# Ranks from one sum of one-hots, places by ScalarE's adding passes, in a graph layer's sorting kernel

## The reference

```python
h    = relu(layernorm(x)) @ W_in2f.T
W    = (smu(edge_attr @ W_f1.T + b_f1) @ W_f2.T + b_f2) * edge_weight[:, None]
agg  = segment_sum(h[dst] * W, src, 12500)
out  = x + smu(agg @ W_o1.T + b_o1) @ W_o2.T + b_o2
```

## Time and profile before

| | |
|---|---|
| median of 3 timed runs | 4130.89 us (4128.15 to 4133.09) |
| the profiled execution's own time | 5828.1 us, which is its span; no time around it is given |
| TensorE products busy in the span | 4390.8 us (75%), 32406 products |
| VectorE busy | 3425.3 us (59%) |
| ScalarE busy | 2120.4 us (36%) |
| GpSimd busy | 3041.4 us (52%) |
| mean granted TensorE clock | 0.825 of full |

### The profile page before, as it was taken

How to read it: one execution, slowest core, us unless ns; L and a number is a source line. 1 busy time by engine, 2 the same in 40 slices (tenths; PEclk the granted TensorE clock), 3 DMA queues, 4 the chain that set the end, 5 groups by cost and what they waited for, 6 DMA issues and landing times.

```text
span 5828.1 us, 115538 instructions
## 1 busy us (share of the span) xinstructions
PE 4390.8 (75%) x32406; PEld 3600.8 (62%) x32406; DVE 3425.3 (59%) x11901; ACT 2120.4 (36%) x7301; POOL 3041.4 (52%) x3173
## 2 busy tenths in 40 slices
PE   5566557777777777777777777777778788778888
PEld 4455446666666666666666666666666666666667
DVE  6555455555565555555555555555656666566667
ACT  3455333333333333333333333333333333333332
POOL 4555555555555555555555555555555555555552
PEclk8777778787888888888788888888888888888899
DMA  5354334444443433433333333333444444445547
GB/s 163 105 134 136 111 109 130 132 130 130 131 122 108 116 112 112 115 115 112 110 113 112 117 112 112 112 111 115 129 132 133 136 141 138 136 135 146 153 143 198
DMA packets 460270, 736.98 MB, mean 126 GB/s; under 512 B 87920, under 2 KB 256218, under 8 KB 459856
## 3 DMA queue, kind: packets, MB, share of 16 engines
q1 hardware_dynamic: 292358, 461.45, 29.9%
q0 software_dynamic: 100000, 206.60, 10.6%
q10 hardware_dynamic: 67626, 65.48, 3.4%
HBM read 465.36 MB, written 267.82 MB: 126 GB/s over the span
## 4 chain that ended last, share of the span: by engine, by line
another core or an unknown queue 34%; PE 32%; issue 14%; DVE 9%; ACT 8%; ACTq 2%; DMA 1%; DVEq 1%; SPq 0%; POOL 0%
PE p_seg L1184 8%; PE p_w L1139 7%; PE p_z L1133 7%; PE p_h L1150 6%; ACT hg L691 3%; DVE product L950 2%; DVE onehot L935 1%; DVE seg_hot L976 1%; PE p_pos L1156 1%; DVE act L926 1%; ACT p_w L705 1%; PE p_pos L1172 1%; ACT gelu L680 1%; ACTq L656 1%
## 5 line engine op out<-in xcount | busy, mean ns | idle before, releaser
L558 POOL DMA_INDIRECT sorted_rows<-msg,row_idx x3125 | 3000.2, 960 | 2697.4 <-DVE msg L943 1799.2
L691 ACT ACTIVATE hg<-p_h,weight 128x128 f32<-128x128 f32 x3136 | 897.2, 370 | 3175.2 <-remote 2840.0
L1184 PEld LDWEIGHTS p_seg<-seg_hot,seg 128*128 128x128 f32 x8288 | 1241.2, 217 | 841.2 <-issue 838.4
L950 DVE CUSTOM_DVE_ANT_0 product<-onehot,p_pos,start_at 128x112 bf16<-128x112 bf16 x3136 | 848.0, 326 | 1456.2 <-remote 1426.4
L1184 PE MATMUL p_seg<-seg_hot,seg 128*128 128x112 f32 x8288 | 1316.4, 303 | 372.8 <-issue 343.1
L1139 PE MATMUL p_w<-w_f,act 128*128 128x128 f32 x6272 | 1155.1, 328 | 250.3 <-issue 245.0
L1139 PEld LDWEIGHTS p_w<-w_f,act 128*128 128x128 f32 x6272 | 989.1, 233 | 265.4 <-issue 263.8
L1133 PE MATMUL p_z<-attr,w_f 128*128 128x512 f32 x1568 | 991.9, 709 | 203.9 <-issue 109.1
L1150 PE MATMUL p_h<-win,pick 128*128 128x128 bf16 x9408 | 836.3, 251 | 284.8 <-ACT hg L691 229.9
L943 DVE TENSOR_TENSOR msg<-p_w,hg 128x512 f32<-128x512 f32 x784 | 540.6, 690 | 717.1 <-ACT hg L691 492.1
L1150 PEld LDWEIGHTS p_h<-win,pick 128*128 128x128 bf16 x9408 | 707.1, 115 | 317.7 <-issue 316.9
(11 more groups left out here) (113 smaller groups left out, 1698.4 us busy)
## 6 DMA issues: line engine op xcount, KB each, us to landing
seg<-sorted_rows SPq DMA_DIRECT2D x560, 322.5 KB
ends<-ends SPq DMA_DIRECT2D x392, 256.0 KB
seg<-sorted_rows SPq DMA_DIRECT2D x112, 516.0 KB
sorted_rows<-msg,row_idx POOLq DMA_INDIRECT x3125
sorted_rows<-zero_rows ACTq DMA_DIRECT2D x336, 129.0 KB
win<-h SPq DMA_DIRECT2D x392, 96.0 KB
attr<-in_attrT SPq DMA_DIRECT2D x392, 80.0 KB
seg<-sorted_rows SPq DMA_DIRECT2D x56, 387.0 KB
```

Source lines behind the costliest of these rows:

```text
L558: pool.indirect_dma_start(out=sorted_rows[:, :], out_offset=bass.IndirectOffsetOnAxis(ap=row_idx[:, slot, k:k + 1], axis=0), in_=msg[:, sl ...
L691: last = act.activation(hg[:, v, k, :], p_h[:, k, :], ACT.Copy, scale=weight[:, bass.ds(n.value(TILES_U, k), 1)])
L950: last = dve.tensor_tensor_reduce(out=product[:, k, :], in0=onehot[:, slot, k, :], in1=p_pos[:, 0:BUCKETS], scale=1.0, scalar=start_at[:, ...
L1184: last = pe.matmul(out, seg[:, it.slot, l * it.tiles + k, 0:F], seg_hot[:, it.slot, l * it.tiles + k, :], start=(k == 0), stop=(k == it.ti ...
```

## The change

Ranks: VectorE sums the four one-hot tiles of a unit, first two and two (`half_sums`), then the halves (`bucket_sums`), and `counted` and `rank` are one product each with this sum. Places: VectorE multiplies all four one-hot tiles by `p_pos` in one instruction (`positions`) into `product`, now fp32 with one more column a tile, into which ScalarE has copied `earlier`. ScalarE then adds each tile's 113 columns by a copying pass with an accumulator output (its new `places`). `bucket_of` goes before `pick_target`, and `row_numbers` behind `message`. On ScalarE, `places(n-1)` stands behind `keys(n-1)`.

```diff
+        product = sb("product", [LANES, 2, TILES_U, BUCKETS + 1])
+        summed = sb("summed", [LANES, 2, TILES_U, BUCKETS + 1])
+        hot_half = sb("hot_half", [LANES, 2, 2, BUCKETS], BF16)
+        hot_sum = sb("hot_sum", [LANES, RING, BUCKETS], BF16)
...
-            def limits(n, slot, rnd):
+            def limits(n, v, slot, rnd):
                 wait_for(act, s_idx, n, 1, 1 - RING)
+                wait_for(act, s_place, n, 1, -1)
                 tiles = bass.ds(n.value(TILES_U), TILES_U)
                 act.activation(place_max[:, slot, :], node_l[:, tiles], ACT.Identity, scale=float(SPACE), bias=last_row[:, rnd:rnd + 1])
-                act.activation(start_at[:, slot, :], earlier[:, tiles], ACT.Copy).then_inc(s_limit, 1)
+                act.activation(product[:, v, :, BUCKETS], earlier[:, tiles], ACT.Copy).then_inc(s_limit, 1)
+
+            def places(n, v):
+                wait_for(act, s_prod, n, 1, 1)
+                wait_for(act, s_limit, n, 1, 1)
+                wait_for(act, s_idx, n, 1, -1)
+                for k in range(TILES_U):
+                    last = act.activation(summed[:, v, k, :], product[:, v, k, :], ACT.Copy, accum_out=place[:, v, k:k + 1])
+                last.then_inc(s_place, 1)
...
                     keys(st.at(1), st.ring(1), st.rnd_of(1))
+                    places(st.at(1), st.v(1))
...
             def bucket_of(n, slot):
-                wait_for(dve, s_rank, n, 1, 2 - RING)
...
+            def half_sums(n, v, slot):
+                wait_for(dve, s_hot, n, 1, 1)
+                dve.tensor_tensor(hot_half[:, v, :, :], onehot[:, slot, 0:2, :], onehot[:, slot, 2:4, :], ALU.add).then_inc(s_half, 1)
+
+            def bucket_sums(n, v, slot):
+                wait_for(dve, s_half, n, 1, 1)
+                wait_for(dve, s_rank, n, 1, 2 - RING)
+                dve.tensor_tensor(hot_sum[:, slot, :], hot_half[:, v, 0, :], hot_half[:, v, 1, :], ALU.add).then_inc(s_hotsum, 1)
+
+            def positions(n, v, slot, half):
                 wait_for(dve, s_rank, n, 1, 1)
-                wait_for(dve, s_idx, n, 1, -1)
-                wait_for(dve, s_limit, n, 1, 1)
-                for k in range(TILES_U):
-                    last = dve.tensor_tensor_reduce(out=product[:, k, :], in0=onehot[:, slot, k, :], in1=p_pos[:, 0:BUCKETS],
-                                                    scale=1.0, scalar=start_at[:, slot, k:k + 1], op0=ALU.mult, op1=ALU.add,
-                                                    accum_out=place[:, v, k:k + 1])
+                wait_for(dve, s_place, n, 1, -1)
+                last = dve.tensor_tensor(product[:, v, :, 0:BUCKETS], onehot[:, slot, :, :],
+                                         p_pos[:, 0:BUCKETS].unsqueeze(1).to_broadcast([LANES, TILES_U, BUCKETS]), ALU.mult)
...
-                last.then_inc(s_place, 1)
+                last.then_inc(s_prod, 1)
...
             def row_numbers(n, v, slot):
                 wait_for(dve, s_place, n, 1, 1)
+                wait_for(dve, s_limit, n, 1, 1)
...
                     smu(st.at(), st.v())
+                    bucket_of(st.at(), st.ring())
                     pick_target(st.at(), st.pair(), st.q(), st.v())
-                    bucket_of(st.at(), st.ring())
+                    half_sums(st.at(), st.v(), st.ring())
...
-                    places(st.at(1), st.v(1), st.ring(1), st.i is None and st.rnd == 0 and st.c == mid_step + 1)
+                    positions(st.at(1), st.v(1), st.ring(1), st.i is None and st.rnd == 0 and st.c == mid_step + 1)
+                if st.has():
+                    bucket_sums(st.at(), st.v(), st.ring())
                 for it in st.items(1):
                     if it.closes:
                         gather_sum(it)
                 if st.has(1):
+                    message(st.at(1), st.v(1), st.ring(1))
                     row_numbers(st.at(1), st.v(1), st.ring(1))
-                    message(st.at(1), st.v(1), st.ring(1))
...
             def counted(slot, rnd):
-                for k in range(TILES_U):
-                    last = pe.matmul(p_pos[:, 0:BUCKETS], not_before[:, :], onehot[:, slot, k, :], start=False, stop=False,
-                                     skip_group_check=True)
-                return last
+                return pe.matmul(p_pos[:, 0:BUCKETS], not_before[:, :], hot_sum[:, slot, :], start=False, stop=False,
+                                 skip_group_check=True)
 
             def rank(n, slot, rnd, opens):
-                wait_for(pe, s_hot, n, 1, 1)
-                wait_for(pe, s_place, n)
+                wait_for(pe, s_hotsum, n, 1, 1)
+                wait_for(pe, s_prod, n)
...
-                for k in range(TILES_U):
-                    last = pe.matmul(p_pos[:, 0:BUCKETS], before[:, :], onehot[:, slot, k, :], start=False, stop=False,
-                                     skip_group_check=True)
-                last.then_inc(s_rank, 1)
+                pe.matmul(p_pos[:, 0:BUCKETS], before[:, :], hot_sum[:, slot, :], start=False, stop=False,
+                          skip_group_check=True).then_inc(s_rank, 1)
```

More of the change, by code:

```diff
@@ L197, in build @@
         place_max = sb("place_max", [LANES, RING, TILES_U])
-        start_at = sb("start_at", [LANES, RING, TILES_U])
         onehot = sb("onehot", [LANES, RING, TILES_U, BUCKETS], BF16)
-        product = sb("product", [LANES, TILES_U, BUCKETS], BF16)
+        product = sb("product", [LANES, 2, TILES_U, BUCKETS + 1])
+        summed = sb("summed", [LANES, 2, TILES_U, BUCKETS + 1])
+        hot_half = sb("hot_half", [LANES, 2, 2, BUCKETS], BF16)
+        hot_sum = sb("hot_sum", [LANES, RING, BUCKETS], BF16)
         stats = sb("stats", [LANES, 2, H_TILES, 6])
@@ L271, in build @@
             sem(n) for n in ("s_z", "s_gelu", "s_smu", "s_w", "s_pick", "s_ph", "s_hg", "s_msg", "s_key"))
-        s_hot, s_rank, s_place, s_idx, s_total, s_count = (
-            sem(n) for n in ("s_hot", "s_rank", "s_place", "s_idx", "s_total", "s_count"))
+        s_hot, s_half, s_hotsum, s_rank, s_prod, s_place, s_idx, s_total, s_count = (
+            sem(n) for n in ("s_hot", "s_half", "s_hotsum", "s_rank", "s_prod", "s_place", "s_idx", "s_total", "s_count"))
         s_seghot, s_seg, s_agg = sem("s_seghot"), sem("s_seg"), sem("s_agg")
@@ L746, in step @@
                         act.wait_ge(s_last, 1)
-                    limits(st.at(), st.ring(), st.rnd)
+                    limits(st.at(), st.v(), st.ring(), st.rnd)
                     add_to_bias(st.at(), st.v())
@@ L943, in message @@
                 dve.tensor_tensor(msg[:, slot, :, 0:F], p_w[v][:, :, :], hg[:, v, :, :], ALU.mult).then_inc(s_msg, 1)
-            def places(n, v, slot, half):
-                wait_for(dve, s_rank, n, 1, 1)
-                wait_for(dve, s_idx, n, 1, -1)
-                wait_for(dve, s_limit, n, 1, 1)
-                for k in range(TILES_U):
-                    last = dve.tensor_tensor_reduce(out=product[:, k, :], in0=onehot[:, slot, k, :], in1=p_pos[:, 0:BUCKETS],
-                                                    scale=1.0, scalar=start_at[:, slot, k:k + 1], op0=ALU.mult, op1=ALU.add,
-                                                    accum_out=place[:, v, k:k + 1])
+            def half_sums(n, v, slot):
[6 more added lines that the diff above has]
+            def positions(n, v, slot, half):
+                wait_for(dve, s_rank, n, 1, 1)
+                wait_for(dve, s_place, n, 1, -1)
+                last = dve.tensor_tensor(product[:, v, :, 0:BUCKETS], onehot[:, slot, :, :],
+                                         p_pos[:, 0:BUCKETS].unsqueeze(1).to_broadcast([LANES, TILES_U, BUCKETS]), ALU.mult)
                 if half:
@@ L1220, in step @@
                 if st.i is None and st.rnd == rounds and st.c == 1:
-                    pe.wait_ge(s_place, n_units)
+                    pe.wait_ge(s_prod, n_units)
                     counted((n_units - 1) % RING, rounds - 1).then_inc(s_total, 1)
```

## The result

The changed kernel takes 4162.72 us (median of 4 runs, 4161.81 to 4164.37), beside the kernel before with 4130.34 us (4 runs, 4128.15 to 4133.09) on the same chip: 1.0077 times as long, 95% interval 1.0064 to 1.0089, or +32 us. The forecast was +145. The sign was right and the time is inside the range, but the forecast case (passes that make the ring slower than GpSimd) did not happen; rival A did, cheap passes with only round 0 showing.

What follows compares the result with a forecast made beforehand. GpSimd's scatters were taken as the bound at 5.05 us a unit. To 4131 us came +108 for the slower steady turn, +33 for round 0 and some +4 for preparation and last units: about 4276, rounded to 4275; range 4136 to 4620.

Steps and rivals of the forecast that it cites:

- the forecast case: ScalarE's adding passes with read at 0.31 to 0.43 us, turn 5.06 to 5.55, 4160 to 4540 us; chance 0.44.
- the ring: VectorE's smu to positions, ScalarE's passes to gelu, back to smu: one unit per 5.24 us turn, taken as 5.2; +108 us.
- rival A: ScalarE passes of 0.2 to 0.3 us, GpSimd's 5.05 holds, only the first round shows: about 4150 us; chance 0.26.
- round 0: Some 48 units where ScalarE also makes h: a pair takes 11.5 us against GpSimd's 10.1, +33 us.
- The bound: GpSimd's scatters, 1.263 us apart, 5.05 us a unit, set the time; what is saved upstream is worth nothing.
- The stretches of 0.7 us: TensorE products 0.7 us apart with 0.45 us of issue before each, taken for the cost of being profiled.
- B: The forecast: ScalarE passes of 0.31 to 0.43 us, at 0.35 4275 us; chance 0.44.
- Last round: Last 16 units, VectorE having 0.3 to 1.3 us more behind its row numbers; with chunk-start preparation some +4 us.
- C: Each ScalarE pass and read run out before the next, 0.45 to 0.53 us: 4600 to 4830 us; chance 0.11.
- D: GpSimd's scatters stretch by VectorE's two sums, at worst 0.48 us a unit: up to 4510 us; chance 0.03.
- E: Not slower: GpSimd stays the bound everywhere, passes under 0.2 us, pair 10.1 to 10.4: 4125 to 4135 us; chance 0.14.
- F: TensorE, with less to do, is granted 1.2 GHz in place of 2.4 for long, 3.97 us becoming 7.9; chance 0.02.

Runs made afterwards that it cites:

- the new order with four passes: Changed kernel with ScalarE's limits and bias copy ahead of the four adding passes: 4165.00 us, 1.0084; 6187.19 us, 1.0453 where the kernel before takes 5914.
- four, five and six passes: Changed kernel as it is (4161.02 us), and with one or two more ScalarE adding passes a unit into a spare tile: 4229.99 and 4448.57 us.
- h was spread: Changed kernel with h made in every third unit of round 0 instead of every second: 4139.81 us, 1.0024.
- ranks alone: Kernel before with the one-hot sums and one product each for counted and rank, places left on VectorE: 4135.37 us, 1.0016; 0.9818 where before takes 5914.
- places alone: Changed kernel with the eight rank products of before and no sums: 4143.18 us, 1.0032; 1.0229 where the kernel before takes 5914.

## Why the forecast was wrong

**The bound: right.** GpSimd's steps of 1.263 us and 5.05 us a unit hold in the profiles of a free chip (in one, the new order with four passes, they are 1.266), and 443 scatters in 560 us of the steady part are the same before and after. That what is saved upstream is worth nothing showed too: TensorE lost 156 us of busy time (3558.3 to 3402.4) and the kernel did not gain.

**The stretches of 0.7 us: wrong.** I took them for the cost of being profiled. They are a condition in which timed runs take 5.9 ms too. The step built on it (compare with the 4111 us) still held, since the timed runs were free of it. "The profiled span says little" fell: the changed kernel's span is its time.

**The ring: right in its members, wrong in its length.** Product, passes, limits, bias copy, gelu and smu follow each other as written, and four, five and six passes show that it is a ring. Its length was forecast at 5.24 us and is 4.78. The step that failed is the price of a pass with its read: 0.35 each against 0.28, 0.27 us of the 0.46. With it fell the sum's largest term, (784 - 48 - 16) x 0.15 = +108 us: the ring stays below GpSimd's unit, and the steady stretch costs less than a scatter. The row ahead of it had the right price: the line through ScalarE's copies (0.185) plus a small operation's 0.095 is 0.28. I moved to the hg passes (0.255), which are 128 elements with a scale read from memory, because I called them the nearest row; a plain Copy was nearer. The other 0.19: VectorE's chain 2.19 and not 2.3 (its 16-bit sums take 0.19 and 0.13, as the low bound had it; the line for the high bound had a slip: smu's 0.60 and onehot's 0.54 leave 0.11 us fixed at 0.96 ns an element and not 0.08, so 0.33 and 0.22 and not 0.29 and 0.19), the wake 0.04 and not 0.1, and the tail 1.42 and not 1.44. It took both errors to pass GpSimd's 5.05: with the true pass and my other terms the sum is 4.97, with my pass and the true others 5.05.

**Steepness: in the ranges, but not said.** From the bend on, 0.01 us a pass is 31 us (784 x 4 x 0.01), so the forecast case's own times ran over 380 us. The chances, 0.44 for B and 0.26 for A, hung on one step of 0.07 us a pass.

**Round 0: right in its mechanism, partly lucky in its number.** Forecast +33, or +20 with passes of 0.28; measured 22 us, and 21 went when h was spread. With such passes the pair was worked out at 10.9 us and is 11.2 in the mean of 23, which alone would give 25 us (23 x 1.1); the lead that GpSimd still has when the stretch begins, which the +20 left out, takes some of it back (an estimate; how much was not measured).

**Last round: missed.** +4 had been put on it and the preparation; it costs 7, and 3 of these come with the sums alone. The ring is not what decides there: in both kernels the chain that ends last runs through TensorE's segment products (39% of it before, 40% after, over the last round's end) and the loading of `attr` (31% in both). What makes it longer in the changed kernel stays open.

**Rivals.** A came true, 2 us over its 10 to 30, with a ring shorter than its 4.9 to 5.0. C fell: the trace has the next pass start 0.28 us behind the last, before the read's 0.19 has run out. The exposed latency of which the Trainium skill, "Advanced Engine Details and Errata", The Read-Write Bubble, warns is not seen in that strict form; a fixed part per instruction agrees with it, since a read of one element still takes 0.09 us until the next pass starts (1208.30 to 1208.39). D came true only in small, 5 us where its worst case was 376: the mean scatter takes 962 ns, and took 960, but the mean hides a few long ones. Scatters of over 0.99 us are 137 in the changed kernel and 118 with ranks alone, but 79 before and 77 with places alone, and in the changed kernel 87% of them, against 17% of the others, run beside a half sum. The pages of ranks alone and of places alone have:

```profile
L560 POOL DMA_INDIRECT sorted_rows<-msg,row_idx x3125 | 3006.1, 962 | 995.3 <-issue 918.3
...
L560 POOL DMA_INDIRECT sorted_rows<-msg,row_idx x3125 | 3000.4, 960 | 1014.2 <-issue 841.7
```

So the kernels with the sums spend some 5 us more in scatters, the two without them do not. The contention in the Trainium skill, "GPSIMD Engine Reference", Key points, agrees with this in kind; that it is the cause is argued from the overlap. The 79 long scatters before, four in five of them beside `pick_target`, show that the sums are not the only partner. E failed by round 0's pair, 11.2 us in the mean where it needed 10.4. F fell: the granted clock is 0.98 of 2.4 GHz from 2000 to 2560 us and 0.90 in the stretch of h (0.95 before). The lower clock is not what costs the 22 us there: the new order with four passes has 0.94 in that stretch and GpSimd is busy for 126.68 us, as in the changed kernel.

No version beat the kernel before. It is 18 us above the 4111 of a GpSimd that never waits, and 6.5 of them are its wait ahead of the last scatter.

## What to carry over

Where one engine bounds the kernel at so much a unit, first draw the ring that a new dependence closes and compare its turn with that unit. Well below it the steady turns cost next to nothing (4.78 against 5.05), at it they already cost something (69 us at 5.06), and behind it 1 for 1, so a forecast near the bend needs its terms to 0.05 us, and the chance belongs on both sides. Price a new operation from the row of the same kind (a copy for a copy), not of the same size. Count the stretches in which the engine has a second job, here h in every second unit of round 0: with a margin of 0.27 us in the steady part it was these that paid, and spreading the second job gave 21 of the 31 us back.

## What the runs showed of the hardware

- An adding pass of ScalarE over 113 elements with its accumulator read takes 0.28 us of its queue, though the two last 0.28 and 0.19 us; turns of a ring with four, five and six of them (4.78, 5.06, 5.35 us) bear it out.
- An indirect scatter of GpSimd's (128 rows) takes 0.96 us and starts 1.263 us behind the last. Where VectorE also adds 16-bit tiles from SBUF (`half_sums`, `bucket_sums`), 118 to 137 of 3125 take over 0.99 us, without that 77 to 79: some 5 us in all, which the mean (962 against 960 ns) hides.
- One program on one set of data took 5914 us at one time and 4129 to 4131 at the others, once on the chip with the same number (medians; the runs of one time lie within 0.4%). In the slower condition TensorE's products come 0.7 us apart or more in stretches (1.46 us in the lines above), with the mean granted clock at 0.82 against 0.97 of 2.4 GHz, and edits rank otherwise: ranks alone takes 0.982 against 1.0016 on a free chip, and the new order with four passes 1.045 against 1.0084. What causes it stays open.
